# Gelu and rounding of the first ffn layer by pairs of slices, with the orders of all engines laid out anew

## The reference, cut to what matters

```python
pooled = x.reshape(Bb, Cc, n, K, n, K).sum(axis=(3, 5))        # 64 x 12 x 14 x 14, 154 MB are read
out = jnp.einsum('bcij,ce->bije', pooled, channel_weights)
h = h + attn(layernorm(h))                                     # softmax(q k^T) v, 192 wide
h = jnp.einsum('bte,he->bth', x, W0) + b0                      # to 768
h = new_gelu(h)
out = jnp.einsum('bth,eh->bte', h, W1) + b1                    # back to 192
```

## Time and profile before

| | us |
|---|---|
| median of 3 runs | 488.52 (488.26 to 488.54) |
| the profiled execution's own time | 490.17 |
| its span | 488.4 |
| PE busy | 427.2 |
| DVE busy | 380.4 |
| ACT busy | 287.0 |
| POOL busy | 255.6 |
| span covered by the chain that ended last, DMA | 46% |

### The profile page before, as it was taken

One profiled execution on the slowest core, in us unless ns is written; L12 is line 12 of the kernel. 1 busy time (PEld: TensorE's weight loads), 2 busy tenths in 40 slices (PEclk: granted clock), 3 DMA queues, 4 the chain that ended last, 5 costly groups with the idle time before them and its releaser, 6 DMA issues.

```text
span 488.4 us, 10938 instructions
## 1 busy us (share of the span) xinstructions
PE 427.2 (87%) x4558; PEld 363.8 (74%) x4558; DVE 380.4 (78%) x272; ACT 287.0 (59%) x478; POOL 255.6 (52%) x194
## 2 busy tenths in 40 slices
PE   5976266986999999989998989899999989999996
PEld 4543144874678889878887878788888878888996
DVE  1688999989899999798989898989999888610000
ACT  1022035623859685849584939586868656877821
POOL 1022314703647582747475838465756575576840
PEclk9999555995599999989999989999999989999999
DMA  8999999999999999999999999999999996001101
GB/s 239 324 405 406 406 406 405 406 408 409 407 404 408 409 407 409 406 402 407 406 410 405 410 407 406 408 402 409 410 409 410 403 407 264 28 26 39 37 26 51
DMA packets 56661, 166.65 MB, mean 341 GB/s; under 512 B 5972, under 2 KB 13030, under 8 KB 56612
## 3 DMA queue, kind: packets, MB, share of 16 engines
q1 hardware_dynamic: 56612, 165.95, 87.2%
HBM read 156.29 MB, written 9.63 MB: 340 GB/s over the span
## 4 chain that ended last, share of the span: by engine, by line
DMA 46%; DVE 23%; PE 18%; SPq 7%; issue 4%; ACT 0%; DVEq 0%
DMA xs<-x 46%; DVE pooled L476 21%; PE ps L604 18%; SPq L408 6%; DVE phat_tok L494 1%; DVE prod L485 0%; ACT out_sb L1018 0%; SPq L425 0%; PE ps L801 0%; DVE var L490 0%; PE ps L781 0%; DVE u_tok L504 0%; PE ps L788 0%; SPq L448 0%; DVE row_inv L502 0%
## 5 line engine op out<-in xcount | busy, mean ns | idle before, releaser
L476 DVE TENSOR_REDUCE pooled<-xs 128x28 f32<-128x1792 f32 x144 | 328.9, 2323 | 28.8 <-DMA xs<-x 28.5
L1116 POOL TENSOR_TENSOR h_lo<-h_f,h_hi 128x784 fp32r<-128x784 f32 x96 | 177.2, 1870 | 74.9 <-ACT h_hi L1012 74.7
L604 PE MATMUL ps<-w_hi,h_hi 128*98 128x192 f32 x768 | 207.7, 270 | 0.5 <-POOL h_lo L1116 0.5
L604 PE MATMUL ps<-w_lo,h_hi 128*98 128x192 f32 x768 | 197.1, 257 | 0.0
L604 PE MATMUL ps<-w_hi,h_lo 128*98 128x192 f32 x768 | 196.7, 256 | 0.0
L604 PEld LDWEIGHTS ps<-w_hi,h_hi 128*98 128x98 f32 x768 | 129.0, 168 | 15.6 <-issue 14.2
L604 PEld LDWEIGHTS ps<-w_lo,h_hi 128*98 128x98 f32 x768 | 129.5, 169 | 0.0
L604 PEld LDWEIGHTS ps<-w_hi,h_lo 128*98 128x98 f32 x768 | 129.2, 168 | 0.0
L1003 ACT ACTIVATE h_f<-ps 128x784 f32<-128x784 f32 x96 | 75.8, 826 | 21.0 <-PE ps L604 20.1
L1012 ACT CAST h_hi<-h_f 128x784 fp32r<-128x784 f32 x96 | 78.4, 856 | 0.0
L1093 POOL TENSOR_TENSOR inv<-var,minus_half 98x8 f32<-98x8 f32 x16 | 26.2, 1639 | 75.9 <-DVE var L490 75.7
(11 more groups left out here) (119 smaller groups left out, 344.9 us busy)
## 6 DMA issues: line engine op xcount, KB each, us to landing
xs<-x SPq DMA_DIRECT2D x336, 448.0 KB, 12.2
out<-out_sb SPq DMA_DIRECT2D x32, 294.0 KB
rows_sb<-wfc SPq DMA_DIRECT2D x1, 576.0 KB, 5.6
out_sb<-wproj SPq DMA_DIRECT2D x1, 576.0 KB, 11.1
h_f<-wqkv SPq DMA_DIRECT2D x1, 432.0 KB
cf<-const_full SPq DMA_DIRECT2D x1, 264.0 KB, 3.1
h_f<-const_paired SPq DMA_DIRECT2D x1, 153.0 KB, 3.5
cr<-const_rows SPq DMA_DIRECT2D x1, 83.2 KB
```

The costliest lines, as they stand in the source:

```text
L476: dve.tensor_reduce(pooled[:, n % 2, t, GRID * first:GRID * end].rearrange("p (i j) -> p i j", j=GRID), runs, AX.XY, ALU.add).then_inc(red ...
L604: return pe.matmul(o, a, b, start=start, stop=stop, skip_group_check=shared)
L1116: pool.tensor_tensor(h_lo[:, m % 2, t], h_f32[:, t], h_hi[:, m % 2, t].bitcast(F32), ALU.subtract).then_inc(h_lo_ready, 1)
```

## The change

Gelu and rounding take two slices in one instruction: 3 + 3 ACT instructions a group in place of 6 + 6. The waits on them change with it: `gelu` of a pair waits for both low parts of the group before, `low_part` waits for the rounding of its pair. POOL keeps its 6 instructions, PE its matmuls. All five tables are new; STEPS, the length of the loop, goes from 4907 to 4958.

```diff
 PE_ORDER = {
-    "sum_rows": (443, 399, 379, 379, 370, 383, 371, 360, 348, 336, 325, 312, 318, 310, 312, 330),
+    "sum_rows": (443, 396, 373, 353, 370, 340, 341, 330, 344, 333, 317, 308, 313, 286, 278, 296),
...
-                    pe.wait_ge(gelu_done, HT * m + 2 * pair)
+                    pe.wait_ge(gelu_done, 3 * m + pair)
...
-            def gelu(m, t):
+            def gelu(m, pair):
                 if m:
 
-                    act.wait_ge(h_lo_ready, HT * (m - 1) + t + 1)
+                    act.wait_ge(h_lo_ready, HT * (m - 1) + 2 * pair + 2)
...
-                act.wait_ge(hidden_summed, 3 * m + t // 2 + 1)
-                act.activation(h_f32[:, t].rearrange("p (b n) -> p b n", b=GROUP),
-                               ps[:, 0:GROUP, TOKENS * (t % 2):TOKENS * (t % 2 + 1)],
+                act.wait_ge(hidden_summed, 3 * m + pair + 1)
+                act.activation(h_f32[:, 2 * pair:2 * pair + 2].rearrange("p t (b n) -> p b t n", b=GROUP),
+                               ps[:, 0:GROUP, 0:2 * TOKENS].rearrange("p b (t n) -> p b t n", t=2),
                                ACT.Gelu_apprx_tanh).then_inc(gelu_done, 1)
...
-                act.copy(h_hi[:, m % 2, t], h_f32[:, t]).then_inc(h_hi_ready, 1)
+                act.copy(h_hi[:, m % 2, 2 * pair:2 * pair + 2], h_f32[:, 2 * pair:2 * pair + 2]).then_inc(h_hi_ready, 1)
...
             def low_part(m, t):
-                pool.wait_ge(h_hi_ready, HT * m + t + 1)
+                pool.wait_ge(h_hi_ready, 3 * m + t // 2 + 1)
```

More of the change, by code:

```diff
@@ L70 @@
 PERIOD = 254
-STEPS = 4907
+STEPS = 4958
 PE_ORDER = {
-    "sum_rows": (443, 399, 379, 379, 370, 383, 371, 360, 348, 336, 325, 312, 318, 310, 312, 330),
[L74 to L82, removed]
+    "sum_rows": (443, 396, 373, 353, 370, 340, 341, 330, 344, 333, 317, 308, 313, 286, 278, 296),
+    "turn_phat": (518, 452, 527, 478, 424, 436, 427, 440, 429, 417, 380, 401, 365, 408, 330, 407),
+    "apply_a": (531, 465, 541, 501, 521, 453, 464, 521, 509, 498, 488, 474, 387, 440, 344, 425),
+    "scores": (545, 596, 565, 559, 585, 558, 563, 542, 531, 519, 510, 504, 490, 482, 469, 455),
+    "turn_maxima": (581, 665, 654, 629, 637, 606, 611, 594, 582, 593, 584, 563, 562, 548, 520, 490),
+    "turned_scores": (595, 680, 668, 658, 651, 621, 626, 609, 598, 609, 599, 579, 577, 564, 536, 505),
+    "weigh": (624, 738, 698, 701, 681, 661, 677, 665, 654, 647, 638, 622, 607, 603, 577, 541),
+    "turn_context": (642, 758, 716, 726, 703, 704, 723, 712, 700, 691, 684, 672, 640, 630, 604, 561),
+    "turn_u": (676, 792, 736, 789, 741, 726, 752, 741, 729, 720, 734, 721, 681, 652, 632, 581),
+    "apply_g2": (689, 804, 761, 818, 766, 748, 770, 759, 747, 738, 753, 740, 705, 686, 651, 600),
@@ L83 @@
     "residual": (
-        (720, 836, 1053, 1046, 1031, 1019, 1007, 996, 984, 972, 960, 960, 928, 924, 893, 828),
-        (970, 1174, 1187, 1157, 1145, 1134, 1122, 1110, 1098, 1086, 1080, 1065, 1032, 1042, 997, 913),
+        (694, 810, 1035, 1094, 1083, 1068, 1057, 1045, 1036, 1021, 1014, 1006, 989, 972, 942, 867),
+        (945, 1177, 1220, 1247, 1194, 1182, 1171, 1164, 1155, 1141, 1133, 1129, 1103, 1080, 1036, 952),
     ),
-    "turn_uhat": (763, 882, 835, 808, 765, 802, 790, 779, 767, 738, 732, 726, 685, 714, 693, 635),
+    "turn_uhat": (733, 893, 835, 876, 829, 826, 823, 811, 822, 813, 797, 791, 766, 744, 706, 661),
@@ L120 @@
 ACT_ORDER = {
[L121 to L131, removed]
-    "gelu": (
[6 rows of a table removed]
+    "load_exp": (360, 583, 454, 555, 583, 545, 529, 558, 547, 535, 526, 524, 484, 476, 455, 442),
+    "copy_p_tok": (455, 406, 383, 385, 380, 368, 351, 340, 354, 343, 327, 318, 323, 296, 288, 309),
+    "copy_phat": (525, 459, 535, 496, 447, 447, 459, 460, 448, 437, 440, 430, 377, 427, 337, 415),
+    "copy_b": (540, 474, 554, 517, 540, 470, 525, 535, 524, 512, 503, 496, 398, 463, 368, 438),
+    "copy_maxima": (590, 674, 663, 638, 646, 615, 620, 602, 591, 602, 593, 572, 571, 557, 529, 498),
+    "exponentials": (608, 694, 681, 671, 664, 635, 639, 623, 611, 622, 613, 592, 591, 577, 549, 518),
+    "load_gelu": (622, 950, 940, 937, 903, 908, 891, 879, 900, 891, 860, 869, 848, 819, 787, 679),
+    "copy_context": (637, 751, 711, 720, 698, 680, 696, 684, 673, 675, 666, 649, 630, 619, 590, 554),
+    "copy_u": (683, 799, 753, 812, 760, 741, 760, 748, 737, 728, 747, 735, 699, 671, 645, 591),
+    "keep_u": (687, 803, 804, 816, 764, 759, 764, 752, 741, 732, 753, 758, 720, 689, 649, 609),
+    "copy_uhat": (741, 901, 842, 884, 838, 833, 830, 819, 830, 820, 805, 798, 774, 751, 730, 669),
+    "gelu": (
[3 rows of a table added]
     ),
     "round_high": (
[6 rows of a table removed]
[3 rows of a table added]
     ),
     "take_out": (
[4 rows of a table removed]
[4 rows of a table added]
     ),
@@ L156 @@
     "reduce": (
[9 rows of a table removed]
-    ),
-    "variance1": (486, 435, 426, 417, 408, 434, 425, 416, 407, 363, 354, 349, 353, 334, 349, 347),
-    "maxima": (581, 662, 556, 574, 545, 556, 527, 518, 509, 501, 495, 474, 475, 436, 464, 443),
-    "context": (694, 804, 746, 697, 653, 673, 664, 656, 652, 647, 608, 601, 582, 609, 596, 549),
-    "variance2": (729, 848, 801, 772, 713, 754, 745, 736, 727, 692, 684, 685, 643, 651, 640, 598),
[9 rows of a table added]
+    ),
+    "variance1": (486, 420, 495, 446, 388, 379, 370, 361, 372, 363, 334, 345, 330, 371, 292, 313),
+    "maxima": (561, 642, 613, 574, 615, 586, 577, 568, 559, 550, 541, 517, 537, 528, 495, 469),
+    "context": (669, 784, 726, 737, 728, 719, 740, 731, 722, 713, 725, 709, 671, 642, 610, 567),
+    "variance2": (699, 859, 801, 841, 783, 774, 785, 776, 767, 758, 762, 754, 725, 702, 660, 609),
 }
 POOL_ORDER = {
-    "scale_p": (493, 442, 433, 424, 415, 441, 444, 432, 421, 371, 362, 356, 367, 341, 368, 370),
-    "scale_u": (738, 857, 810, 781, 736, 776, 765, 753, 740, 713, 707, 700, 655, 682, 666, 607),
+    "scale_p": (493, 427, 503, 454, 395, 403, 377, 368, 380, 371, 342, 353, 338, 378, 300, 321),
+    "scale_u": (709, 869, 810, 851, 805, 800, 797, 786, 777, 770, 771, 764, 739, 714, 669, 630),
     "low_part": (
[6 rows of a table removed]
[6 rows of a table added]
     ),
@@ L185 @@
     "load": (
[9 rows of a table removed]
[9 rows of a table added]
     ),
     "send": (
-        (1066, 1272, 1285, 1255, 1244, 1231, 1220, 1208, 1196, 1180, 1176, 1163, 1130, 1140, 1095, 1011),
-        (1188, 1405, 1398, 1379, 1367, 1355, 1343, 1332, 1319, 1308, 1312, 1276, 1275, 1243, 1180, 1096),
+        (1055, 1287, 1329, 1346, 1298, 1285, 1274, 1266, 1257, 1251, 1235, 1239, 1210, 1190, 1146, 1062),
+        (1152, 1395, 1458, 1446, 1432, 1421, 1409, 1400, 1383, 1378, 1370, 1353, 1335, 1306, 1231, 1147),
     ),
@@ L739, in scores @@
                 if m == 1:
-                    pe.wait_ge(gelu_done, HT)
+                    pe.wait_ge(gelu_done, 3)
                 elif m == 2:
@@ L743, in scores @@
                 elif m:
-                    pe.wait_ge(gelu_done, HT * (m - 1))
+                    pe.wait_ge(gelu_done, 3 * (m - 1))
                 for h in range(2):
@@ L813, in hidden @@
                     else:
-                        pe.wait_ge(gelu_done, HT * m)
+                        pe.wait_ge(gelu_done, 3 * m)
                 else:
-                    pe.wait_ge(gelu_done, HT * m + 2 * pair)
+                    pe.wait_ge(gelu_done, 3 * m + pair)
                 for t in (2 * pair, 2 * pair + 1):
@@ L993, in copy_uhat, with round_high @@
                          ps[:, MB, 0:TOKENS].rearrange("p (n h) -> p n h", h=2)).then_inc(uhat_rows_ready, 1)
-            def gelu(m, t):
+            def gelu(m, pair):
                 if m:
-                    act.wait_ge(h_lo_ready, HT * (m - 1) + t + 1)
+                    act.wait_ge(h_lo_ready, HT * (m - 1) + 2 * pair + 2)
                 if m == 0:
                     act.wait_ge(setup_pool, POOL_W1)
-                act.wait_ge(hidden_summed, 3 * m + t // 2 + 1)
-                act.activation(h_f32[:, t].rearrange("p (b n) -> p b n", b=GROUP),
-                               ps[:, 0:GROUP, TOKENS * (t % 2):TOKENS * (t % 2 + 1)],
+                act.wait_ge(hidden_summed, 3 * m + pair + 1)
+                act.activation(h_f32[:, 2 * pair:2 * pair + 2].rearrange("p t (b n) -> p b t n", b=GROUP),
+                               ps[:, 0:GROUP, 0:2 * TOKENS].rearrange("p b (t n) -> p b t n", t=2),
                                ACT.Gelu_apprx_tanh).then_inc(gelu_done, 1)
-            def round_high(m, t):
-                act.wait_ge(gelu_done, HT * m + t + 1)
-                if m >= 2 and t == 0:
+            def round_high(m, pair):
+                act.wait_ge(gelu_done, 3 * m + pair + 1)
+                if m >= 2 and pair == 0:
                     act.wait_ge(out_summed, 4 * (m - 1))
-                act.copy(h_hi[:, m % 2, t], h_f32[:, t]).then_inc(h_hi_ready, 1)
+                act.copy(h_hi[:, m % 2, 2 * pair:2 * pair + 2], h_f32[:, 2 * pair:2 * pair + 2]).then_inc(h_hi_ready, 1)
```

(10 more changed lines are left out.)

## The result

| | before | changed |
|---|---|---|
| median, us | 488.39 (486.94 to 488.54, 4 runs) | 493.86 (493.02 to 495.28, 4 runs) |
| profiled execution, its span | 490.17, 488.4 | 493.74, 492.0 |
| PE, DVE, ACT, POOL busy | 427.2, 380.4, 287.0, 255.6 | 427.1, 379.6, 282.2, 255.4 |

The ratio is 1.012, with a 95% interval of 1.0088 to 1.0152: slower. The spans differ by only 3.6 us because the profiled execution of before was 1.8 us above its median, and the changed one was at its own.

A forecast was written before the change was run, and what follows sets the result against it. Memory was taken to bound the kernel up to gate 14 (sum_rows of group 14), then PE's remaining matmuls. 7.6 us more behind that gate, added to the 488.52 us median, gave 496.1 us, range 491.5 to 501.

The forecast's parts named there:

- The rule: A gate is a group's sum_rows on PE, waiting for reduced pixels; PE's end is at least its time plus matmuls behind.
- The term of 7.6 us: Extra matmul work behind gate 14 in PE's list, 856 before and 934 after: 7.6 us; behind gate 15, 7.8 us.
- I take 393.35: Gate 14, sum_rows of group 14, closed by the memory, was claimed to open at the same time, 393.35 us.
- Gate 15 gives no more ... PE comes to gate 15 at about 421.: At gate 15, DVE's possible gain of 3 us was claimed lost, since PE arrives only at about 421 us.
- The sum: Gate 14 to PE's end grows from 91.4 to 99.0 us; 7.6 us added to the median gives 496.1 us.
- The merge: On ACT, paired gelu and rounding save about 0.2 us a group, nothing on the path; POOL's 0.6 us delay is hidden.
- rival (b): The merge delays POOL and PE by 0.6 us for each of the last three groups: 497.9 us, chance 0.10.
- SP and the loads: SP's sends at other places may hold loads back; cost nothing, as transfers are issued 11 us or more before landing.
- PE's idle time between 140 and 393 us grows from 15.3 by about 7 us.: Sign expected in the changed profile: PE idles about 7 us more before gate 14, over 15.3 us.
- (a): Rival: the tail gets new stalls, or loads are held behind sends; 499 to 503 us, chance 0.13.
- (c): Rival: no change, since the matmuls are the same; 488.5 us, needing gate 14 at 385.8; chance 0.04.
- (d): Rival: faster, as ACT's saved 1.5 us is on the path; 487.0 us, needing gate 14 by 385.8; chance 0.05.

The follow-up runs named there:

- experiment 11: Changed kernel with DVE reducing the last chunk of pixels twice, so gate 15 (sum_rows of group 15) opens 2.95 us later: 496.29 us, ratio 1.0181.
- Experiments 9: Kernel before with sum_rows of groups 3, 5 and 6 alone at the changed kernel's steps: 487.3 us, ratio 0.9989.
- 12: Kernel before with DVE reducing the last chunk of pixels twice, 2.95 us added ahead of gate 15: 491.77 us, ratio 1.0092.
- Experiments 4: Kernel before with four projections of group 11 (24 matmuls) moved from behind gate 14 to ahead of it: 488.5 us, ratio 1.0000.
- experiment 1: Kernel before, its tables kept, with gelu and rounding of each pair merged at the second slice's place: 489.57 us, ratio 1.0033.
- experiments 7: Kernel before with pixel transfers from the third tile on cut to 64 of 128 partitions: 475.1 us, ratio 0.9735.
- 8: Changed kernel with pixel transfers from the third tile on cut to 64 of 128 partitions: 480.99 us, ratio 0.9846.
- 6: Changed kernel with sum_rows of group 15 moved behind 40 more matmuls, leaving 644 instead of 684 behind gate 15: 497.89 us, ratio 1.0207.
- 3: Kernel before with sum_rows of group 15 moved ahead of 56 matmuls in PE's list, 660 behind gate 15: 498.75 us, ratio 1.0221.
- 10: Kernel before with the whole sum_rows row of steps from the changed kernel, 636 matmuls behind gate 15: 500.7 us, ratio 1.0254.
- 5: Changed kernel with four projections of group 11 (24 matmuls) moved from behind gate 14 to ahead of it: 493.38 us, ratio 1.0117.

## Why the prediction was right, and where it was off

**The rule.** "PE cannot end before a gate's time plus all matmuls behind the gate" holds in every run, and it gave the sign. The size was 7.6 us in the forecast and 5.5 in the medians. The 80 matmuls more behind gate 15 are the loss: with the full or the halved input, every run with 604 behind it has a tail of 63.6 us (64.3 with the merge), every run with 684 one of 70.2 to 70.4.

**The term of 7.6 us** was mis-sized. It is 6.74 us at gate 15, where I had 7.8. By unit prices 80 matmuls are 7.8 us; the tail has 0.4 us less idle (1.6 to 1.2), and the rest of about 0.6 us lies in the small delays between units, which I did not resolve further.

**"I take 393.35" for gate 14.** It was passed at 391.95. In the twelve profiles with the full input its last reduction ended between 390.97 and 393.50, whichever the lists, so 1.4 us is within the scatter of profiled executions and not shown to be an effect of the change. Taking one execution's gate as fixed cost me 1.4 us. My reason was right in kind: PE waited there, 1.79 us, and the last reduction had followed its landing at once. But of the 9.4 us that I saw in hand there only these 1.79 were left: PE had lost the others in waits before.

**"Gate 15 gives no more ... PE comes to gate 15 at about 421."** This is the step that failed, by 3 us. It rested on the 27.76 us between the gates in the profile of before, of which 3.41 us ran at a clock of 0.51 and cost 1.7. The changed kernel had no such stretch, took 26.00 us, and PE was there at 417.87 (experiment 11). So DVE's 3 us were not lost: held back by 2.95 us, they cost 2.4. I had the 1.7 us in the low end of the range and not in the forecast. Experiments 9 and 12 show that before's list can do without such a stretch: at a clock of 1.00, its PE was at gate 15 at 419.0 and 418.5.

**The sum.** Against the profiles: 99.0 us from gate 14 to the end were forecast and 96.36 measured, -1.7 for the clock and -0.9 for the term, and the gate itself was 1.4 earlier: together the 4.0 us between 492.35 and 488.31. Against the medians I was off by 2.2 us only, because I had added the 7.6 to a median that was 1.65 below the profile; that part of the closeness is luck. The profile of before, with its slow stretch, is also why the spans show 3.6 us and the medians 5.5. Experiments 4 and 9 took 488.52 and 488.17 us in their profiled executions, near before's median. Against them the changed kernel passes gate 15 by 1.5 and 1.1 us earlier and has a tail 6.7 longer: 5.2 and 5.7 us.

**The merge**, worth nothing by my sum and 1.8 us by rival (b), costs 1.6 us on before's tables and nothing that can be told on the changed ones. There the prediction's "hidden" is right; on before's tables it is not. The Trainium skill, "Perfetto Trace Analysis", section "Optimizing Scalar/DVE Operations", says that where the Scalar or Vector engine isn't saturated but causes bubbles on others, breaking instructions up may let work be completed sooner; experiment 1, with its new waits of 1.09 and 0.45 us for POOL, agrees.

**SP and the loads** cost nothing: SP waits 91.8 us at the sends where it waited 83.0, and the transfers still run at 407 GB/s from 140 us to gate 14. The prediction took the DMA share of 1.03 as its evidence; experiments 7 and 8 show that this share says little, the rate does.

**"PE's idle time between 140 and 393 us grows from 15.3 by about 7 us."** It grew to 251.95 - 235.02 = 16.9. The 7 us are there, but earlier, between 90 and 190 us (6.8 us, above). I had looked only at what follows 140 us.

**The rivals.** (a) new stalls in the tail: not in the changed kernel (1.2 us idle), though moving a gate gave one in 6 (3.7 us idle); in 3 and 10 the tail has 1.6 us idle as before and the half clock on top. (c) and (d) needed gate 14 at 385.8; no run with the full input has it.

What stays open: why PE is late at gate 14 in some profiles (in 4, by 3.3 us) and waits there in others; why the small delays between units are 0.6 us less in the changed tail; how often an execution of before has the stretch at half clock behind gate 14; and whether a list with 604 behind gate 15, together with the changed DVE list, would win, which wasn't run.

## What to carry to other kernels

Where a late input closes an in-order engine's list, count what stands behind the last such wait: total work did not tell these versions apart, and filling the earlier wait moved the end in neither of two runs (4 and 5). Treat a gate's time and the length between two gates as ranges over executions, and take stretches at half clock out of a length before you reuse it. And look which engine closes the gate: if its list makes it wait for the very engine that waits at the gate, with long work behind that wait, a small slip comes back larger (10: 3.1 us of matmuls, 13 us in the end).
